# Taking the groups of the node stage in another order on VectorE, TensorE and ScalarE in a graph network

## The reference, cut to what matters

```python
agg = segment_sum(msg * alpha, dst)          # sum of weighted messages / sum of weights
out = h + agg
z = relu(layernorm(out @ w1 + b1, g1, bb1))  # 64 -> 128 channels
conv = z @ w2 + b2                           # 128 -> 64 channels
h = h + conv
z_next = relu(layernorm(h, g, b))            # the table that the next layer gathers from
```

## Time and profile before

| | |
|---|---|
| median of three runs | 8966.54 us |
| the profiled execution | 8967.96 us |
| its span, first to last instruction | 8966.2 us |
| busy: PE, VectorE (DVE), ScalarE (ACT), GpSimd (POOL) | 12%, 71%, 36%, 71% of the span |
| mean granted clock of TensorE | 0.521 of full speed |
| one node stage, from the first L1158 to the end of the last L1195 | 139.6 to 139.8 us, four times |

### The profile page before, as it was taken

The page is one execution under the profiler, slowest core; times in us unless marked ns, Lnnn a source line. Parts: engine busy times, 40 slices in busy tenths (PEclk is TensorE's granted clock), DMA queues, the critical chain, the costliest instruction groups (busy, mean ns, idle before and its releaser), DMA issues.

```text
span 8966.2 us, 43989 instructions
## 1 busy us (share of the span) xinstructions
PE 1074.9 (12%) x3019; PEld 778.9 (9%) x3019; DVE 6407.4 (71%) x10611; ACT 3236.4 (36%) x7064; POOL 6370.8 (71%) x6739
## 2 busy tenths in 40 slices
PE   4333333332100000000210000000020000000003
PEld 3222222221100000000100000000020000000002
DVE  7777777776577777777657777777756777777775
ACT  3444444443333333333333333333333333333332
POOL 6777777776477777777557777777746777777773
PEclk6555565555555555555555555555555555555555
DMA  6666666663244444444234444444423444444442
GB/s 193 202 200 206 205 203 201 204 204 123 70 142 138 136 136 139 140 137 136 92 89 136 136 139 141 137 136 136 141 74 102 138 141 138 136 136 141 139 137 66
DMA packets 439687, 1288.07 MB, mean 144 GB/s; under 512 B 159659, under 2 KB 173652, under 8 KB 361812
## 3 DMA queue, kind: packets, MB, share of 16 engines
q1 hardware_dynamic: 221668, 1049.13, 32.2%
q0 software_dynamic: 217968, 238.47, 13.1%
HBM read 575.00 MB, written 712.10 MB: 144 GB/s over the span
## 4 chain that ended last, share of the span: by engine, by line
DVE 24%; POOL 19%; DMA 14%; issue 10%; ACT 6%; PE 3%; DVEq 0%; POOLq 0%; ACTq 0%; SPq 0%
POOL gathered L501 18%; DMA gathered<-node_table,idx_s 13%; DVE rows_out L1070 5%; DVE run L1060 3%; DVE track L1030 3%; DVE run L1056 3%; DVE psum L1018 3%; DVE psum L1048 3%; DVE psum L1043 3%; ACT track L700 2%; ACT psum L707 1%; PE psum L610 1%; PE psum L627 1%; DVE psum L1158 1%; ACT psum L721 1%
## 5 line engine op out<-in xcount | busy, mean ns | idle before, releaser
L501 POOL DMA_INDIRECT gathered<-node_table,idx_s x6464 | 6102.9, 944 | 2243.0 <-issue 1892.7
L714 ACT ACTIVATE decay<-psum 128x512 f32<-128x512 f32 x808 | 482.6, 597 | 4935.6 <-DVE psum L1043 4935.6
L1010 DVE STREAM_TRANSPOSE psum<-gathered 128x512 f32<-128x512 f32 x808 | 576.8, 714 | 2140.6 <-DMA gathered<-node_table,idx_s 2140.3
L1030 DVE TENSOR_TENSOR_SCAN track<-psum,track,edges 128x256 f32<-128x256 f32 x1616 | 1110.1, 728 | 0.0
L1056 DVE TENSOR_TENSOR_SCAN run<-decay,run,psum 128x256 f32<-128x256 f32 x1616 | 1102.1, 721 | 0.0
L1060 DVE TENSOR_TENSOR_SCAN run<-decay,run,psum 128x256 f32<-128x256 f32 x1616 | 1097.0, 720 | 0.0
L1070 DVE STREAM_TRANSPOSE rows_out<-run 128x1024 f32<-128x1024 f32 x808 | 971.3, 1202 | 0.6
L543 PE MATMUL psum<-attr_s,edgew_s 128*128 128x256 f32 x1616 | 746.0, 641 | 1242.2 <-ACT made_s L646 1225.5
L700 ACT ACTIVATE track<-psum,bias_col 128x256 f32<-128x256 f32 x1616 | 679.6, 471 | 213.5 <-DVE psum L1018 163.4
L588 PE MATMUL psum<-cst,tails 128*3 128x128 f32 x48 | 10.9, 414 | 6208.9 <-DVE tails L1109 6128.2
L543 PEld LDWEIGHTS psum<-attr_s,edgew_s 128*128 128x128 f32 x1616 | 500.8, 325 | 1485.9 <-ACT made_s L646 1355.4
(11 more groups left out here) (167 smaller groups left out, 1513.2 us busy)
## 6 DMA issues: line engine op xcount, KB each, us to landing
edge_state<-rows_out SPq DMA_DIRECT2D x404, 1024.0 KB, 10.8
edges<-edge_rows SPq DMA_DIRECT2D x406, 640.0 KB
tracks<-track SPq DMA_DIRECT2D x404, 513.0 KB
gathered<-node_table,idx_s POOLq DMA_INDIRECT x6464, 2.8
edge_rows<-made_s SPq DMA_DIRECT2D x101, 640.0 KB, 9.6
attr_s<-in_attr SPq DMA_DIRECT2D x101, 512.0 KB, 10.5
made_s<-resets SPq DMA_DIRECT2D x101, 128.0 KB
node_table<-tab SPq DMA_DIRECT2D x27, 224.0 KB, 2.4
```

Of the source, the lines that this page charges most:

```text
L501: pool.indirect_dma_start(gathered[u][:, at:at + C], None, table, bass.IndirectOffsetOnAxis(ap=idx_s[u][:, col:col + 1], axis=0)).then_inc ...
L1010: v.transpose(turned[s].rearrange("p (q b e) -> p b q e", q=2, e=LANES), gathered[u][:, W * st:W * st + W]).then_inc(turn_done, 1)
L1030: last = v.tensor_tensor_scan(maxima[u][:, at:at + N], logit[s][:, N * q:N * q + N], reset_s[u][:, N * st:N * st + N], carried[:, RUN * q ...
```

## The change

The functions stay as they are, but for one, which is split; the loops call them in another order. On VectorE the reciprocal of the sums leaves `aggregate` and becomes `invert_sums(i)`, with the hold on the gathered rows and a new wait on VectorE's own earlier work on `quot_ps` (`tab_ready` of group i-3, or `pre_ready` of group i-1 where i is 1 or 2); it is called first in a step. `aggregate(i)` now follows `invert_hidden(i-1)`, and `add_conv(i-2)` comes behind it. On TensorE `turn_norm(i-1)` moves between `turn_pre(i)` and `hidden(i)`, and the matmuls of w2 run for group i-1 at the end of the step, where they ran for group i-2 at its start. On ScalarE the squares of group i, `spread_hidden(i)`, end step i, where they began step i+1, and `copy_pre(i)` goes ahead of `spread_h(i-2)`.

```diff
@@ TensorE
-                for i in range(NODE_GROUPS + 2):
-                    if i >= 2:
-                        conv(i - 2)
+                for i in range(NODE_GROUPS + 1):
                     if i < NODE_GROUPS:
                         turn_pre(i)
+                    if i >= 1:
+                        turn_norm(i - 1)
+                    if i < NODE_GROUPS:
                         hidden(i)
-                    if 1 <= i <= NODE_GROUPS:
-                        turn_norm(i - 1)
+                    if i >= 1:
+                        conv(i - 1)
@@ ScalarE
                 for i in range(NODE_GROUPS + 2):
                     if 1 <= i <= NODE_GROUPS:
-                        spread_hidden(i - 1)
                         scale_hidden(i - 1)
+                    if i < NODE_GROUPS:
+                        copy_pre(i)
                     if i >= 2:
                         spread_h(i - 2)
-                    if i < NODE_GROUPS:
-                        copy_pre(i)
                     if 1 <= i <= NODE_GROUPS:
                         relu_norm(i - 1)
+                    if i < NODE_GROUPS:
+                        spread_hidden(i)
@@ VectorE
-                def aggregate(i):
+                def invert_sums(i):
                     n, w = layer * NODE_GROUPS + i, WIDTHS[i]
                     hold(v, dve_passed, ends_part[i], 16 * w * (layer + 1))
                     rows = ends[:, FIRST[i]:FIRST[i] + w, :]
                     q = quot_ps[:, 0:w * C].rearrange("p (t c) -> p t c", c=C)
+                    if i >= 3:
+                        v.wait_ge(tab_ready, n - 2)
+                    elif i >= 1:
+                        v.wait_ge(pre_ready, n)
                     v.reciprocal(q, rows[:, :, 0:C]).then_inc(quot_steps, 1)
+
+                def aggregate(i):
+                    n, w = layer * NODE_GROUPS + i, WIDTHS[i]
+                    rows = ends[:, FIRST[i]:FIRST[i] + w, :]
+                    q = quot_ps[:, 0:w * C].rearrange("p (t c) -> p t c", c=C)
                     v.wait_ge(quot_steps, 2 * n + 1)
...
                 for i in range(NODE_GROUPS + 2):
+                    if i < NODE_GROUPS:
+                        invert_sums(i)
                     if 1 <= i <= NODE_GROUPS:
                         invert_hidden(i - 1)
-                    if i >= 2:
-                        add_conv(i - 2)
                     if i < NODE_GROUPS:
                         aggregate(i)
                     if i >= 2:
+                        add_conv(i - 2)
                         next_table(i - 2)
```

## The result

The changed kernel takes 8753.94 us (median of four runs, 8749.44 to 8758.3) against 8965.87 before: a ratio of 0.9764, 95% interval 0.9752 to 0.9776, 212 us less.

The account below looks back on a forecast made before the run. No engine was full; engine order alone chained parts of different groups into one 18.79 us ring. 11.7 + 10.0 + 4 x 10.37 + 9.3 + 7.0 + 10.5 = 90.0 a stage, from 139.7, gave 8767 us, range 8735 to 8793.

Parts of the forecast that it names:

- The ring: Node stage, new order: the chain through TensorE from one group's rstd1 to the next sets the step, 10.37 us.
- The size of a step: Node stage, seven-tile group: 10.37 us between neighbouring rstd1, bounds 10.2 and 10.7, in place of 18.79.
- VectorE's ring: Node stage: VectorE's work in one step, with its waits, takes 9.9 us, 10.2 at most, just below the longest ring.
- The root: In VectorE's ring: the root of the variances on ScalarE and back takes about 0.36 us.
- The start: Node stage: first rstd1 comes 11.7 us after the start, before 9.63; the change costs 2.1 here.
- The end of a stage: Node stage, from the last rstd1 to the end of the table: 10.5 us, its chain stays.
- the two narrow steps: Node stage, late steps: 9.3 us for the six-tile group, 7.0 for the last of four tiles.
- the first step: Node stage, from group 0's rstd1 to group 1's: 10.0 us, with its copy uncovered.
- Rival 2: TensorE's clock rises in the node stages: some 6.5 us less a stage, 8741, or 8755 if half the time; chance 0.33.
- the first rival: The forecast itself: the ring through TensorE sets a step of 10.4 us; 8767, own range 8755 to 8780; chance 0.53.
- Rivals 3 to 5: Node stage: VectorE becomes the bound, 8798, chance 0.09; old ring stays, 8967, 0.02; late gathers make it slower, 9029, 0.03.
- rival 5: Node stage: a late gather stops the older group's chain on VectorE; 9029 at 3.0 us a gather; chance 0.03.

Follow-up runs that it names:

- e1: The changed kernel with VectorE's loop back in the old order; 10398.4 us, 0.9917 of the kernel before on the same chip.
- e2: The changed kernel with TensorE's loop back in the old order; 10345.89 us, 0.9870 of the kernel before on the same chip.
- e3: The changed kernel with ScalarE's loop back in the old order; 10290.32 us, 0.9822 of the kernel before on the same chip.
- e10: The kernel before with only VectorE's loop in the new order; 8846.79 us, 0.9863 of the kernel before on the same chip.
- e4: The changed kernel with a copy in place of the reciprocal of the sums (output differs); 10262.57 us, 0.9787 of the kernel before on the same chip.
- e5: The changed kernel with the matmuls of w2 done twice; 8770.65 us, 0.9779 of the kernel before on the same chip.
- e8: The changed kernel with ScalarE's squares beginning after the first four tiles of hidden; 8744.48 us, 0.9750 of the kernel before on the same chip.
- e6: The changed kernel with group 0's rstd1 ahead of the reciprocal of group 1's sums; 8761.8 us, 0.9769 of the kernel before on the same chip.
- e11: The changed kernel with squares after four tiles and a copy for the sums' reciprocal (output differs); 8717.43 us, 0.9719 of the kernel before on the same chip.

## Why the prediction was right

**The ring.** What the prediction named is what the chain of waits shows after: `pre`, L602, L619, L610, squares and root, and w2 and relu out of it. e1, e2, e3 and e10 put the single pieces back and found each ring about where its sum had it (5.4 us in front of the product; 12.49; 10.77; 13.25), but for e1's whole step, which the clock made shorter than its sum. e4, which leaves the step at 10.13, shows that this ring, not VectorE's, sets it at 1.2 GHz.

**The size of a step.** 10.13 against 10.37. The term that was off is `hidden(i)`: 3.2 taken, 3.00 measured, the lower bound given. The block of w1 takes 0.36 less behind the transposes than after a gap; a block of transposes takes 0.18 less behind another block. The other terms came within 0.03. The matmuls of w2 of group i-1 were said to be over some 0.9 after `rstd1`, with 0.6 to spare:

```profile
8699.05 3.09 PE L627 MATMUL psum<-w2c_s,normT 128*128 128x64 f32 x14
```

They are over 0.46 after `rstd1` at 8701.68, and TensorE's next work is there at 8703.23, so 1.1 are to spare.

**VectorE's ring, just below.** 9.9 was said. It shows in steps of 9.87 in the first stage and in e5, where the clock had risen, and of 9.94 in e8, there at a clock of 0.50. That the sum fits is in part luck, as two terms were off in opposite directions. The new wait on the table costs less than the 0.15 taken: L1164 starts 8708.67 - 8708.63 = 0.04 after the end of L1206, near the lower bound of 0.03. The root costs more than the 0.36 taken, 0.59 of idle time ahead of L1198: it stands behind `copy_pre(i)` on ScalarE, as the prediction allowed for.

**The start.** 11.3 against 11.7, as the second group's rows land 8.43 after the first reciprocal and not 8.7. The sum was right, the reading as a price of the change was not (e6).

**The end of a stage** is, with the full steps, the term that was furthest off: 10.5 taken, as "its chain stays", and 9.3 to 9.9 measured. In the last stage of before, h of group 6 starts 1.41 after the last `rstd1` (8946.53):

```profile
8947.94 0.56 DVE L1173 TENSOR_TENSOR h<-psum,h 128x384 f32<-128x384 f32 x1 [1.23 <-PE psum L627]
```

In the second stage of the changed kernel run again, with the clock at 0.50, it starts 0.84 after it:

```profile
4417.22 0.18 DVE L1179 RECIPROCAL rstd<-dev 128x4 f32<-128x4 f32 x1 [0.58 <-ACT dev L765]
4418.06 0.56 DVE L1184 TENSOR_TENSOR h<-psum,h 128x384 f32<-128x384 f32 x1 [0.66 <-PE psum L627]
```

That is 0.57 earlier, and the end is shorter by as much, 9.94: w2 of group 6 now follows `hidden` of group 7 at once, where it had to wait for the transposes and the relu of its own group. The chain behind it stays, through h, the root and `relu_norm` of the last group. With the clock risen just there (8738.16 - 8738.07 = 0.09) this chain is out of the way, and the end is 9.28. I read this from the timelines and the chains of waits; no run isolates it.

**The sum.** In that stage at a clock of 0.50, 88.1 us long, the start is 0.4 below the forecast, the four full steps 0.6 together, the two narrow steps 0.3 and the end 0.6; the first step is as said. So the forecast was high by 1.9 a stage for reasons that have nothing to do with the clock.

**The clock.** Rival 2 came in part: 0.50 to 0.62 in a stage. A stage at 0.50 takes 88.1, at 0.52 to 0.54 some 87, at 0.62 86.2: 1 to 2 us of the 6.5 that were set for a clock risen throughout. So of the 13 us by which the forecast was high, about half are the clock and the rest the terms of the sum: 90.0 was said, 88.1 measured at 1.2 GHz, 86.6 on the mean. The time alone would not have told the first rival from the second: 8753.9 lies a little below the range set for the first (8755 to 8780) and near the 8755 set for the second with the clock up half the time. The steps of 10.13 at a clock of 0.50 tell them apart.

**Rivals 3 to 5.** VectorE's waits do not add 0.5 at three places (0.04 at the table, 0.23 more than taken at the root); the old ring is gone; the gathers are not late. The mechanism of rival 5, a step that waits for gathered rows, does appear in e11, once the step falls to their pace of 8.7. The gathers take 945 ns on the mean, as before, with VectorE busy 72% of the stage.

## What to carry to other kernels

Where engines take work in a written order, look in the chain of waits for stretches of *different* groups that follow each other without needing each other's data; then write down every ring of the new order with durations from the old trace, as the next one may lie only 0.2 us below (here 10.13, 9.9 and 8.7). Shortening the longest ring is worth little more than the distance to the next: e8 alone gained 15 us on the changed kernel, and with VectorE's ring cut too (e11) it is some 40, by the ratios. Work put behind an earlier wait is not a cost by itself: ask whether the same time comes back on the other side of it.

## What the runs showed of the hardware that was not expected

**The clock went with the order on TensorE.** In every kernel with TensorE's old order (before, e2, e10) the granted clock is 0.50 in all node stages, also in e10, where TensorE is busy 69.3 of 109 us. In every kernel with the new order it rises to 1.00 for stretches in nearly all stages (not in the second stage of the changed kernel run again, nor in that of e6), also in e1, where TensorE is busy 54 of 153 us: 0.76 on the mean of the 14 us from 10310 on. In the new order the transposes, w1 and w2 of a full step follow each other without a gap, for 9.0 us where the clock is at 0.50. In the old one w1 and the transposes behind it do so for 4.9, and w2 comes after a gap. So the orders differ in two things, in what stands next to w1 and in how long TensorE works without a gap, and no run here separates them. What the Trainium skill (TensorE: Matmul & The Clock Gate, Part 4: PE-mode transpose) says, that transposes do not count as busy in the same way, would make the first the one that matters; no run here took the transposes alone. More matmuls can then cost nothing in a stage: with w2 twice the clock went to 0.65 to 0.78, and the first of the four stages got shorter, though the kernel as a whole took 11 us more.

**One chip was slower by 17%.** The kernel before takes 10485 us there and some 8967 on the others. In e1, e3 and e4 the squares (L761) wait 131 to 145 us in all, once in each of the four node stages, for something that the profile puts outside the core; in e2 the step is as long. That is a tenth of the 1518 us. The rest is in the edge stages: in e4 the one between the first two node stages lasts 2403 us, in the changed kernel 2073, and there too waits are put outside the core. The cause stays open. The full steps and the gains in us agree with the rings all the same.
